# First pass of a graph network kernel: step lists fetched by aligned fours a unit ahead, sums in front of the dense steps, the gathered rows added by TensorE

## The reference, cut to what matters

```
h = relu(layernorm(x))
msg  = relu(h[src] + edge_attr_16 @ We + be)          # layer 0: the first pass over the edges
x    = x + gelu((h + segment_sum(msg, dst)) @ W1 + b1) @ W2 + b2
# layer 1: ten steps h = 0.9 * A h + 0.1 * h0, A from edge_weight and the degrees of src and dst
# layer 2: three layers with edge attention; layer 3: one edge layer with silu
```

## Time and profile before

| | |
|---|---|
| median of 3 runs | 5066.88 us (5066.79 to 5070.62) |
| profiled execution | 5063.05 us |
| its span | 5061.2 us |
| PE busy | 3352.0 us, 66% |
| DVE busy | 2802.1 us, 55% |
| POOL busy | 3017.2 us, 60% |
| ACT busy | 936.6 us, 19% |

### The profile page before, as it was taken

The page is one execution under the profiler, slowest core; times in us unless marked ns, Lnnn a source line. Parts: engine busy times, 40 slices in busy tenths (PEclk is TensorE's granted clock), DMA queues, the critical chain, the costliest instruction groups (busy, mean ns, idle before and its releaser), DMA issues.

```text
span 5061.2 us, 80463 instructions
## 1 busy us (share of the span) xinstructions
PE 3352.0 (66%) x19803; PEld 2150.1 (42%) x19804; DVE 2802.1 (55%) x9539; ACT 936.6 (19%) x3266; POOL 3017.2 (60%) x3058
## 2 busy tenths in 40 slices
PE   1221026666666668999997788768886787856666
PEld 1220003222222233333334666656665666635554
DVE  7951035555555542111115888768886888865554
ACT  0000002222222210000001222222221222211221
POOL 3887763333333368888202777647773777737776
PEclk9999998788787879999997999879997999955555
DMA  4311122222222259999993222322222222221112
GB/s 142 96 26 15 9 68 54 51 50 55 52 55 53 55 123 333 363 354 347 366 345 122 62 62 62 52 55 62 61 63 44 62 62 62 62 23 28 28 28 30
DMA packets 293562, 511.57 MB, mean 101 GB/s; under 512 B 169174, under 2 KB 207203, under 8 KB 291962
## 3 DMA queue, kind: packets, MB, share of 16 engines
q1 hardware_dynamic: 118407, 353.77, 19.7%
q0 software_dynamic: 92160, 115.72, 12.6%
q10 hardware_dynamic: 82800, 40.01, 2.7%
HBM read 449.40 MB, written 58.97 MB: 100 GB/s over the span
## 4 chain that ended last, share of the span: by engine, by line
POOL 38%; PE 29%; issue 17%; DVE 6%; DVEq 4%; DMA 3%; ACT 1%; SPq 0%; POOLq 0%; ACTq 0%
POOL arena L736 29%; PE ps L1460 28%; POOL rows_dst L721 9%; DVEq L490 3%; DVE arena L1065 1%; DMA arena<-table,arena 1%; DVE arena L1049 1%; PE ps L1632 1%; DMA arena<-in_edge_attr_dram 1%; DVEq L1045 1%; DMA arena<-rows_dst 1%; PE ps L1594 1%; DVE arena L1045 1%; ACT arena L1396 0%; DVE nodes L790 0%
## 5 line engine op out<-in xcount | busy, mean ns | idle before, releaser
L736 POOL DMA_INDIRECT arena<-table,arena x2080 | 2016.0, 969 | 1706.6 <-DMA arena<-rows_dst 1015.9
L1460 PE MATMUL ps<-arena 128*128 128x96 f32 (+3 forms) x9176 | 1641.6, 359 | 946.9 <-DVE arena L1049 394.8
L1460 PEld LDWEIGHTS ps<-arena 128*128 128x128 f32 (+3 forms) x9176 | 1064.2, 200 | 1539.8 <-issue 1245.3
L1460 PE MATMUL ps<-arena,nodes 125*64 125x500 f32 (+3 forms) x3504 | 702.9, 542 | 41.2 <-DVEq L1154 16.2
L721 POOL DMA_INDIRECT rows_dst<-stage,arena x400 | 485.6, 1214 | 196.7 <-issue 121.6
L1065 DVE TENSOR_SCALAR arena<-iota_row_b,arena 128x128 f32<-128x128 bf16 x2080 | 586.6, 300 | 0.0
L694 POOL DMA_INDIRECT rows_src<-stage,stage_at x400 | 484.7, 1212 | 116.8 <-issue 107.2
L1045 DVE SCALAR_TENSOR_TENSOR arena<-iota_row_b,arena 128x384 bf16<-128x384 bf16 x572 | 349.4, 611 | 228.5 <-issue 226.3
L1077 DVE TENSOR_TENSOR arena<-ps,arena 128x256 f32<-128x256 f32 x416 | 176.6, 424 | 518.3 <-DMA arena<-table,arena 504.8
L1064 DVE TENSOR_SCALAR arena<-iota_row_b,arena 128x128 bf16<-128x128 bf16 x1664 | 457.7, 277 | 6.3 <-PE ps L1460 2.4
L1460 PEld LDWEIGHTS ps<-arena,nodes 125*64 125x64 f32 (+1 forms) x3504 | 266.3, 137 | 434.4 <-issue 413.4
(11 more groups left out here) (280 smaller groups left out, 3342.4 us busy)
## 6 DMA issues: line engine op xcount, KB each, us to landing
arena<-dense SPq DMA_DIRECT2D x360, 750.0 KB, 7.2
dense<-arena ACTq DMA_DIRECT2D x150, 250.0 KB, 3.0
arena<-table,arena POOLq DMA_INDIRECT x2080
arena<-rows_dst SPq DMA_DIRECT2D x208, 96.0 KB
arena<-pair_rows SPq DMA_DIRECT2D x12, 976.6 KB
arena<-dense SPq DMA_DIRECT2D x6, 1750.0 KB, 18.9
rows_dst<-stage,arena POOLq DMA_INDIRECT x400
rows_src<-stage,stage_at POOLq DMA_INDIRECT x400
```

The costliest lines, as they stand in the source:

```text
L736: nc.gpsimd.indirect_dma_start(rows[:, u, k, 0:width], None, frm, bass.IndirectOffsetOnAxis(ap=p[:, c, j, c_other:c_other + 1].bitcast(I32 ...
L1460: return nc.tensor.matmul(to, lhsT, rhs, start=start, stop=stop, skip_group_check=True)
```

## The change

The tables are read in groups of four whose first place is a multiple of four. `fours` gives an engine a `fetch(i, u)` that loads the groups which unit u needs and no earlier unit has loaded; the values stay in registers. A body has 11 groups a table. `fetch` for u+1 stands behind the dense steps of u; at u = 0 the unit's own fetch stands in the turn itself. `need` is read without the bounds check, and each value is raised to at least one in the queue.

On PE the gathered rows are added to `lin` by a product with the identity, so PE now waits for `gathered[u]`. `lin` and the transposed payload alternate between banks 4 and 5 by unit. `sum_up` of u-2 stands ahead of the dense steps of u. DVE's add and its wait on `sum_ready` are gone; it takes the relu straight from PSUM into `msg`. PE waits for `msg_ready` of u-1 before it transposes the payload of u+1, in place of `sum_ready`. At the end of the pass DVE raises `sum_ready` by the 104 that later passes count on.

```
+        def lin(u):
+            return ps[:, 4 + u % 2, 0:K * D].rearrange("p (k d) -> p k d", k=K)
+        def payT0(v_):
+            return ps[0:K * C, 4 + v_ % 2, K * D:K * D + 128]
...
+        def first_step(u):
+            return u // 2 * PER2 + u % 2 * PER_U[0]
+        def fours(eng, tables):
+            held_values = {}
+            def fetch(i, u):
+                lo_, hi_ = first_step(u) // 4, (first_step(u) + PER_U[u % 2] - 1) // 4
+                for q in range(lo_, hi_ + 1):
+                    if u == 0 or q > (first_step(u) - 1) // 4:
+                        for name, (table_, lowest, highest) in tables.items():
+                            values = load_values(eng, table_[0:1, bass.ds(i * PER_BODY + 4 * q, 4)], lowest, highest)
+                            for k in range(4):
+                                held_values[name, 4 * q + k] = values[k]
+            return held_values, fetch
...
             def turn0(i, u, before, more):                              # DVE
+                if u == 0:
+                    fetch_operands(i, u)
                 ...
                 dense_operands(i, u)
+                if u + 1 < U:
+                    fetch_operands(i, u + 1)
                 if more:
                     turn_keys(i, u + 1)
                 v.wait_ge(lin_ready, i * U + (u + 1))
-                v.wait_ge(gathered[u], 16 * K * (i + 1))
-                nc.vector.tensor_tensor(of(s1, u)[:, 0], lin, rows[:, u, :, 0:D], ALU.add).then_inc(sum_ready, 1)
-                v.wait_ge(sum_ready, i * U + (u + 1))
-                nc.vector.tensor_scalar(of(msg, u)[:, :, 0:D], of(s1, u)[:, 0], 0.0, None, ALU.max).then_inc(msg_ready, 1)
+                nc.vector.tensor_scalar(of(msg, u)[:, :, 0:D], lin(u), 0.0, None, ALU.max).then_inc(msg_ready, 1)
             over_units(v, turn0)
+            v.sem_inc(sum_ready, NB * U)
...
             def dense_steps(i, u):                                      # PE
-                banks = load_values(pe, bank_of[0:1, bass.ds(at_, n)], DB0 * 512, (DB0 + EV - 1) * 512)
-                needs = load_counts(pe, need[0:1, bass.ds(at_, n)], 1, BINS)
-                for k in range(n):
+                if u == 0:
+                    fetch_steps(i, u)
+                first = first_step(u)
+                for k in range(PER_U[u % 2]):
                     slot = (first + k) % PER2
-                    hold(pe, bank_free, needs[k])
-                    pe.wait_ge(op_ready, at_ + (k + 1))
+                    pe.reg_alu(at_least_one, step_at["need", first + k], 1, ALU.max)
+                    hold(pe, bank_free, at_least_one)
+                    pe.wait_ge(op_ready, i * PER_BODY + (first + k + 1))
                     ...
+                if u + 1 < U:
+                    fetch_steps(i, u + 1)
...
             def turn0(i, u, before, more):                              # PE
                 ...
                 if more:
-                    turn_payload(i, u + 1, 5)
-                if before:
-                    pe.wait_ge(sum_ready, i * U + u)
-                mm(ps[:, 4, 0:K * D], of(payT, u), wl0[:].rearrange("p k d -> p (k d)")).then_inc(lin_ready, 1)
-                dense_steps(i, u)
+                    if before:
+                        pe.wait_ge(msg_ready, i * U + u)
+                    turn_payload(i, u + 1, payT0(u + 1))
+                mm(ps[:, 4 + u % 2, 0:K * D], of(payT, u), wl0[:].rearrange("p k d -> p (k d)"))
+                pe.wait_ge(gathered[u], 16 * K * (i + 1))
+                mm(lin(u), ident[:], rows[:, u, :, 0:D], start=False).then_inc(lin_ready, 1)
                 if before == 2:
                     sum_up(i, i, u - 2, 1)
+                dense_steps(i, u)
```

More of the change, by code:

```diff
@@ L206, in gnn_kernel @@
         used[0] = KEEP_FROM
+        assert KEEP_FROM % 4 == 0 and TABLE_W % 4 == 0 and PER_BODY % 4 == 0
         bank_of = carve([1, TABLE_W], I32)
@@ L1033, in _ @@
             flat_keys = rel_key.rearrange("p g t -> p (g t)")
+            operand_at, fetch_operands = fours(v, {"tile": (tile_of, 0, T - 1), "key": (key_of, 0, CG * T - 1)})
             def dense_operands(i, u):
[L1037 to L1041, removed]
[L1042 removed]
+                first = first_step(u)
+                for k in range(PER_U[u % 2]):
                     slot = (first + k) % PER2
[L1044 removed]
+                    tile_at, key_at = operand_at["tile", first + k], operand_at["key", first + k]
+                    v.wait_ge(built, i * PER_BODY + (first + k + 1))
                     nc.vector.scalar_tensor_tensor(
[L1046 to L1047 removed]
+                        lhs[:, slot], iota_row_b[:].unsqueeze(1).to_broadcast([128, 3, 128]), lo_col[:, bass.ds(tile_at, 1)],
+                        w_parts[:, bass.ds(tile_at, 1), :].rearrange("p o c -> p (o c)").unsqueeze(2).to_broadcast([128, 3, 128]),
                         ALU.is_equal, ALU.mult)
[L1049 removed]
+                    nc.vector.tensor_scalar(rhs[:, slot, :], iota_col_h[:], flat_keys[:, bass.ds(key_at, 1)], None,
                                             ALU.is_equal).then_inc(op_ready, 1)
@@ L1091, in turn_keys @@
                 v.wait_ge(tr_ready, i * U + (v_ + 1))
-                nc.vector.tensor_copy(of(payT, v_), payT_ps(5)).then_inc(payT_ready, 1)
+                nc.vector.tensor_copy(of(payT, v_), payT0(v_)).then_inc(payT_ready, 1)
             def turn0(i, u, before, more):
+                if u == 0:
+                    fetch_operands(i, u)
                 if before == 0:
@@ L1522, in load4 @@
                 return load_values(pe, at_, lowest, highest)
+            step_at, fetch_steps = fours(pe, {"bank": (bank_of, DB0 * 512, (DB0 + EV - 1) * 512), "need": (need, 1, BINS)})
+            at_least_one = pe.alloc_register("at_least_one")
             def dense_steps(i, u):
-                first = u // 2 * PER2 + u % 2 * PER_U[0]
-                at_ = i * PER_BODY + first
-                n = PER_U[u % 2]
-                banks = load_values(pe, bank_of[0:1, bass.ds(at_, n)], DB0 * 512, (DB0 + EV - 1) * 512)
-                needs = load_counts(pe, need[0:1, bass.ds(at_, n)], 1, BINS)
-                for k in range(n):
+                if u == 0:
+                    fetch_steps(i, u)
+                first = first_step(u)
+                for k in range(PER_U[u % 2]):
                     slot = (first + k) % PER2
-                    hold(pe, bank_free, needs[k])
-                    pe.wait_ge(op_ready, at_ + (k + 1))
+                    pe.reg_alu(at_least_one, step_at["need", first + k], 1, ALU.max)
+                    hold(pe, bank_free, at_least_one)
+                    pe.wait_ge(op_ready, i * PER_BODY + (first + k + 1))
                     for part in range(3):
-                        ins = mm(flat[:, bass.ds(banks[k], CW)], lhs[:, slot, part, :], rhs[:, slot, :], start=False, stop=False)
+                        ins = mm(flat[:, bass.ds(step_at["bank", first + k], CW)], lhs[:, slot, part, :], rhs[:, slot, :], start=False, stop=False)
                     ins.then_inc(built, 1)
+                if u + 1 < U:
+                    fetch_steps(i, u + 1)
             def clear(ep):
@@ L1552, in load_unit, with turn_payload @@
                 return load4(table_[0:1, side, bass.ds(i * BODY + v_ * K, K)], 0, highest)
-            def turn_payload(m, v_, bank):
+            def turn_payload(m, v_, to):
                 c = v_ % U // UC
@@ L1558, in turn_payload @@
                 j = v_ * K % CT
-                nc.tensor.transpose(payT_ps(bank), pay[:, c, j:j + K, :].rearrange("p k c -> p (k c)"), ident[:]).then_inc(tr_ready, 1)
+                nc.tensor.transpose(to, pay[:, c, j:j + K, :].rearrange("p k c -> p (k c)"), ident[:]).then_inc(tr_ready, 1)
             def sum_up(i, m, v_, side):
```

7 lines of the change are left out of this document (3 added, 4 removed).

## The result

The changed kernel took 4703.79 us (median of 4 runs, 4700.37 to 4714.92), the kernel before 5066.84 us beside it (4 runs, 5057.11 to 5070.62). The ratio is 0.9293, 95% interval [0.9282, 0.9304]: 363 us less, where 490 were forecast. It lies inside the range, 127 us above the forecast, 13 us from the rival "POOL starves" (4717) and 3 us from the rival "The clock stays where it is" (4707).

The account below looks back on a forecast made before the run. A PE–DVE chain was taken to bound the first pass at 10.96 us a unit; DVE's 5.8 plus 0.45 gave 6.25 (PE 5.35, POOL 5.6), saving 490 us over 104 units: 4577 us, range 4520 to 4750.

Parts of the forecast that it names:

- POOL starves: Rival, first pass: with DVE never quiet each gather doubles to 1.9 us, 7.6 us a unit, 4717 us; chance 0.11.
- The clock stays where it is: Rival, first pass: PE's clock stays at 0.81, giving 7.5 us a unit, 4707 us; chance 0.12.
- The bound before and the chain: First pass: no engine full; a chain between PE and DVE sets 10.96 us a unit, 4.5 of it two DVE waits.
- Loads in aligned fours: DVE and PE list reads: four aligned numbers cost 0.34 us, fetching 1.25 us a unit on each queue.
- Fetch beside running operands: DVE's queue: loads for u+1 are covered by operands still running; without that cover they cost 1.25 us a unit.
- DVE's and TensorE's own work: First pass, work a unit: DVE 5.8 us, PE 5.35 us at full clock.
- GpSimd's term: First pass: four gathers of 1.39 us, 5.6 us a unit, the excess over 0.95 growing with DVE's share.
- the wait that I priced at nothing: PE's wait for gathered rows before the add: no cost; if POOL became slower, every engine would go at its pace.
- the prediction's own signs of being wrong: First pass: gathers' mean over 1.5 us or PE waiting for arena<-table; clock near 0.8; DVE "issue" idle; long bank-refill waits.
- locked out: Rival, first pass: full DVE stretches every gather to 3.11 us, 13.6 us a unit, 5346 us; chance 0.04.
- The 0.45 us for ties: First pass, added a unit for three near-equal engines: body edges 0.15, PE's bare fetch, and banks 0.1.

Follow-up runs that it names:

- b1: Kernel before, with only the step lists fetched by aligned fours a unit ahead: 5928.06 us, ratio 0.9642.
- b2: Kernel before, with only sum_up put in front of the dense steps: 5933.14 us, ratio 0.9654.
- b3: Kernel before, with both aligned fours and sum_up in front, DVE still adding the gathered rows: 5783.01 us, ratio 0.9411.
- x1: Changed kernel with the two-input operand write (L1068) of each dense step replaced by a memset, dense matrix left out: 4603.01 us, one run.
- x2: Changed kernel with the one-input operand write (L1072) of each dense step replaced by a memset, dense matrix left out: 4614.24 us, one run.
- e9: Changed kernel with the two-input operand write replaced by three one-input tensor_scalars, same numbers: 5829.66 us, ratio 0.9417.
- e5: Changed kernel with the aligned fours undone: exact lists read where used, need checked: 5952.08 us, ratio 0.9643.
- e4: Changed kernel with sum_up of u-2 again behind the dense steps: 5908.9 us, ratio 0.9556.
- e8: Changed kernel with ScalarE reading its bin ends without the bounds check: 5818.23 us, ratio 0.9414.
- e2: Changed kernel with DVE's two PSUM readings (payT copy, relu) moved between its dense operands, same numbers: 4649.28 us, ratio 0.9187.
- e11: Changed kernel with DVE's two PSUM readings between its dense operands and ScalarE's bin ends read unchecked: 5784.86 us, ratio 0.9414.
- e1: Changed kernel with one gather a unit instead of four in the first pass, other rows zero: 4607.24 us, ratio 0.9101.

## Why the prediction was off by a quarter of the gain

**The bound before and the chain: right.** The pass was a chain, not an engine at its limit, and its three waits went nearly as said: 245.5 us of one-hots to 33.2, 226.3 us of "issue" to none, 394.8 us of TensorE's wait to 34.9. b1, b2 and b3 show that either link alone gives some 60% of what both give.

**Loads in aligned fours: right.** 0.332 and 0.342 us in the median, forecast 0.34, and 142 or 143 a table. The Trainium skill's 0.2 us a register ("Runtime: NRT & Kernel Launch", "Instruction fetch mechanics") would be 0.8 us a load, and neither of these medians is near it.

**Fetch beside running operands: right.** L1068 and L1072 have no idle time before them in the pass.

**DVE's and TensorE's own work: right where nothing disturbs them.** There DVE's units follow at 5.33 us (five steps) and 6.11 (six), mean 5.72; I had 5.8. The relu from PSUM takes 0.415 us for 0.41. TensorE's two products begin 0.44 us apart (1077.42 and 1077.86, clock 1.00), as priced. Over the whole pass TensorE is busy 627.18 / 104 = 6.0 us a unit, not 5.35; part of it is the clock, which came to 0.93 and not above 0.95, the rest I did not take apart.

**The step that failed: GpSimd's term.** I priced a gather at 1.09 us, by letting the excess over the quiet 0.95 grow with DVE's busy share. It measured 1.574. The excess does not follow how busy DVE is: b1 and b2 have the same share, 28 and 1 gathers over 3 us, and means of 1.34 and 1.08. It comes from a second kind of gather, which beside a run of dense operands does not end before the run does, and which needs the two-input write (x1, x2, e9). In the layer pass DVE is 81% busy and the median gather is 0.95 us, which I read as proof against starving; there, two-input writes from SBUF come at most two in a row. The runs of five or six steps stood in the kernel before too, just as unbroken, with one gather in 409 held. Why the changed kernel's gathers are caught so much more often, and b1's more often than b2's, is not shown. It goes with the fours: without them 1 (before, b2) and 6 (e5) gathers last over 3 us, with them 18 to 57 (b3, b1, e4, e8 and the changed kernel), unless the PSUM readings stand between (e2 7, e11 6).

4 x (1.574 + 0.30) = 7.50 us is above every other term, and the wait that I priced at nothing cost what the prediction said it would "if POOL became the slower one". Two of the prediction's own signs of being wrong are there: a mean over 1.5 us, and PE waiting for `arena<-table`. What happened is the rival "POOL starves" (chance 0.11) in its mechanism, gathers stretched by DVE. That its 7.6 us a unit and 4717 lie near the measured 7.44 and 4703.8 is in part luck: it doubles the gather to 1.9 us and leaves out the 0.30 us between two gathers, which the forecast's own term and the rival "locked out" count. With it, it would have said 8.8 us. The rival "The clock stays where it is" came nearer still, 4707, and by luck alone: the clock rose to 0.93. The row that spoke for starving stood in the earlier trace rows, a gather of 3.11 us, and the prediction used it only for the far rival "locked out".

**The 0.45 us for ties: half of what was needed.** With the gathers out of the way the pace is 6.55 to 6.65 us a unit (x1, e1), not 6.25. One part is seen. At ten of the pass's body edges DVE waits for "issue" before its weight copy, 40.9 us in all and up to 5.0 each (the same in e1, 39.5 us). One of them:

```profile
1129.25 0.28 DVE L1115 COPY arena<-ps 96x128 f32<-96x128 f32 x1
1129.45 0.41 DVE L1131 TENSOR_SCALAR arena<-ps 128x256 f32<-128x256 f32 x1
1133.35 0.17 DVE L1083 COPY arena<-arena 128x4 f32<-128x4 f32 x1 [3.49 <-issue]
```

The branch of the loop was issued at 1127.88, the queue's next instructions stand at 1131.20, 3.3 us later, and four loads follow in the open. The ten edges are 40.9 / 104 = 0.39 us a unit where 0.15 was forecast; I had counted the loads and not the branch. The kernel before has the same silence, 2.7 to 3.3 us at each of these edges. The rest I put down, without a run that shows it, to TensorE's waits for a bank (16.2 us are seen, others are hidden in its queue), behind ACT's read and check of seven bin ends once in a block row, 1.64 us and seven times over 0.16. e8 was to show it and could not, so this part stays open.

So of the 1.19 us a unit between 7.44 and 6.25, 0.79 are the gathers (7.44 against e1's 6.65). The other 0.40 are what the edges and the open part cost beyond the 0.45 allowed. Times 104 units the 1.19 us are 124 us of the 127 missed.

The Trainium skill, "SBUF — State Buffer", section "Who interferes with whom", says that a VectorE instruction with two inputs in SBUF contends with a GpSimd instruction that reads SBUF. By that rule the gathers, which read their indices there, suffer from L1068; x1, x2 and e9 agree for the gathers of over 3 us. It also names `tensor_scalar` in its 2-port mode as one that locks GpSimd out for a whole instruction. Whether any `tensor_scalar` here ran in that mode no trace tells; they speak neither clearly for the sentence nor against it: with one-input writes of 0.23 us no gather exceeds 1.11 us (x1), with those of e9 gathers reach 1.85 us. In the prediction I weighed only the second of these two sentences.

## What to carry to other kernels

A mean over a few long cases and many short ones is no price that grows gently: ask what makes the long case long, and what the time would be if it became common. Here a gather issued by GpSimd takes 0.95 us when it is left alone and up to 5.8 us beside VectorE's two-input writes, and the share of the long ones followed neither VectorE's busy share nor the pace. Spreading the PSUM-reading instructions among those writes adds no instruction, made the long ones rare (7 for 57) and gave half of the time expected. A chain that goes to and fro between two engines can be cut at either link, and the second cut gives less than the first: each alone gave 216 to 221 us and both 366. Read small tables in aligned fours, a unit ahead, and look at the loop's branch too, where 3.3 us of silent queue came on top. And do a rival's sum as carefully as the forecast's: one here was near the result because it left a term out.

## What the runs showed of the hardware that was not expected

- Beside back-to-back dense operands gathers come in two kinds: one lasts to the run's end (5.80 us beside six steps, 3.11 beside three; all 57 over 3 us end 0.81 or 0.82 us behind the last operand); the other ends inside the run after 0.94 to 1.34 us (117). In e2 a gather lasted 5.77 us across two PSUM-reading instructions.
- Beside one-input writes alone gathers lasted up to 1.85 us (e9), 51 of 409 over 1.5 us.
- Fewer gathers don't get shorter ones: with one a unit the mean was 2.50 us.
- Behind a loop's backward branch VectorE's queue was silent for 2.8 to 3.7 us at the ten body edges of the changed kernel's pass.
- Chips differ: the same kernel before took 5060 us on one and 6149 and 6172 on two others, with register instructions of 0.05 us lasting up to 0.73 us there.
